# A fused attention, expert and scan layer on Trainium2: the scan norm adds its two halves on GpSimd, and every order list is replaced

## The reference

```
x = x + attention(LN(x))      # 16 heads of 8; elu(q)+1, elu(k)+1; weights = (rope q . rope k) / (q . k); no softmax
x = x + experts(LN(x))        # router, 2 of 8 experts, 512 hidden, exact gelu, plus a shared expert
x = x + scan(LN(x))           # 256 inner channels, 16 states
x = x + experts(LN(x))        # the same experts again
```

```
xc = silu(conv(W_in x));  dt = softplus(W_dt xc + b)
h  = exp(dt * A[s]) * h + dt * B[s] * xc       # for each of 16 states s, over time
y  = sum over s of C[s] * h
mu = mean(y);  var = mean((y - mu)**2)          # over the 256 channels
y  = (y - mu) * rsqrt(var + 1e-5) * ln_g + ln_b
out = W_out ((y + xc * D) * silu(z))
```

## Time and profile before

| | us |
|---|---|
| Median of 3 runs (lowest, highest) | 3752.46 (3748.87, 3768.64) |
| The profiled execution's own time | 3761.18 |
| Its span, first to last instruction | 3759.4 |
| PE busy | 3412.8 (91%) |
| ACT busy | 3189.4 (85%) |
| DVE busy | 2658.9 (71%) |
| POOL busy | 1330.1 (35%) |
| Granted TensorE clock, mean | 0.949 of full speed |

### The profile page before, as it was taken

The page is one execution under the profiler, slowest core; times in us unless marked ns, Lnnn a source line. Parts: engine busy times, 40 slices in busy tenths (PEclk is TensorE's granted clock), DMA queues, the critical chain, the costliest instruction groups (busy, mean ns, idle before and its releaser), DMA issues. The chain is left out here.

```text
span 3759.4 us, 38374 instructions
## 1 busy us (share of the span) xinstructions
PE 3412.8 (91%) x11446; PEld 1450.4 (39%) x11446; DVE 2658.9 (71%) x3527; ACT 3189.4 (85%) x4024; POOL 1330.1 (35%) x744
## 2 busy tenths in 40 slices
PE   5886999999999999999999999999999999998847
PEld 1231434444343444434343444434344343434424
DVE  4438768686776868687786868778686867768572
ACT  4776889999999999899999999899999989886643
POOL 0122434244343424334242434434243443315251
PEclk6796999999999999999999999999999999999968
DMA  5433445454545545464544545454454545434332
GB/s 161 122 84 110 138 152 157 140 179 134 178 136 163 163 132 182 128 196 138 159 151 147 174 134 178 143 159 151 140 174 138 182 146 163 149 108 165 117 128 76
DMA packets 214847, 552.01 MB, mean 147 GB/s; under 512 B 25105, under 2 KB 96626, under 8 KB 214642
## 3 DMA queue, kind: packets, MB, share of 16 engines
q1 hardware_dynamic: 212914, 547.99, 47.2%
q10 hardware_dynamic: 1728, 1.57, 0.1%
HBM read 488.65 MB, written 63.18 MB: 147 GB/s over the span
## 5 line engine op out<-in xcount | busy, mean ns | idle before, releaser
L938 PE MATMUL bank<-hF,wst 128*128 128x512 f32 x2304 | 1149.6, 620 | 30.4 <-ACT hF L1040 15.6
L1525 POOL TENSOR_TENSOR yM<-yM,ws 128x1024 f32<-128x1024 f32 x240 | 634.3, 2643 | 1410.4 <-DVE ws L1422 1407.2
L1303 DVE TENSOR_TENSOR rPool<-bank,rPool 128x512 f32<-128x512 f32 x1024 | 700.1, 686 | 550.4 <-PE bank L866 440.5
L1040 ACT ACTIVATE hF<-bank,cols 128x512 f32<-128x512 f32 x1152 | 772.3, 687 | 259.4 <-PE bank L927 245.3
L1194 ACT ACT_TABLE_LOAD x518 | 664.6, 1283 | 9.2
L1040 ACT ACTIVATE rPool<-bank 128x512 f32<-128x512 f32 x1024 | 571.9, 597 | 93.9 <-PE bank L861 87.5
L925 PE MATMUL bank<-xnH,wst 128*128 128x512 f32 x1152 | 605.4, 526 | 30.7 <-ACT hF L1040 20.2
L1415 DVE TENSOR_TENSOR_SCAN ws<-dAs,ws 128x1024 f32<-128x1024 f32 x256 | 600.9, 2353 | 7.4 <-ACT dAs L1040 0.8
L938 PEld LDWEIGHTS bank<-hF,wst 128*128 128x128 f32 x2304 | 419.9, 193 | 463.5 <-issue 364.2
L866 PE MATMUL bank<-qpk,kpk 48*128 48x512 bf16 x1024 | 412.2, 405 | 94.0 <-DVE rPool L1303 85.7
L1040 ACT ACTIVATE rPool<-rPool 128x2048 f32<-128x2048 f32 x256 | 490.4, 1916 | 2.3
(11 more groups left out here) (162 smaller groups left out, 2934.6 us busy)
## 6 DMA issues: line engine op xcount, KB each, us to landing
wst<-wscr SPq DMA_DIRECT2D x288, 768.0 KB, 5.8
bc<-bcscr SPq DMA_DIRECT2D x256, 512.0 KB, 4.4
cB<-gscr SPq DMA_DIRECT2D x256, 256.0 KB, 4.6
kpk<-kscr SPq DMA_DIRECT2D x128, 192.0 KB, 5.5
qpk<-qscr SPq DMA_DIRECT2D x128, 192.0 KB, 5.9
qscr<-parts SPq DMA_DIRECT2D x186, 128.0 KB, 2.2
kscr<-parts SPq DMA_DIRECT2D x186, 128.0 KB, 2.3
wscr<-wst SPq DMA_DIRECT2D x9, 512.0 KB, 6.2
```

What stands on the lines that cost most here:

```text
L938: pe.matmul(ps[FFN][:, :], w2, hF[:, (NCH * f + q) % HSLOTS, :], start=(c == 0), stop=(c == FC - 1)).then_inc(s_dn, 1)
L1040: return nc.scalar.activation(out_, in_, fn, **kw)
L1303: v.tensor_tensor(rP[:, slot, c, :], ps[num_bank(b, s)][:, :], rP[:, slot, c, :], ALU.mult).then_inc(s_mul, 1)
L1525: g.tensor_tensor(yM[:, :, :], yM[:, :, :], ws[:, s % 3, :, :], ALU.add).then_inc(s_ya, 1)
```

## The change

In the 15 norms of the passes 2 to 16, POOL adds the two halves first, and PE sends only the sum through `onesI`, for the mean and again for the variance. The sum goes to the first half of `sqE`. The last norm (pass 17) stays as it was. A new semaphore `s_E_half` counts the sums.

```
             def scan_norm(m, i, name):                       # PE
+                last = isinstance(i, int) and i == NB + 1
                 if name == "mean":
-                    pe.wait_ge(s_ya, floor((NS - 1) * (m + 1)))
+                    if last:
+                        pe.wait_ge(s_ya, (NS - 1) * NB)
+                    else:
+                        pe.wait_ge(s_E_half, floor(2 * m + 1))
...
-                    ones_mm(PRE, onesI, [yM[:, 0, :], yM[:, 1, :]], 2).then_inc(s_E_mean, 1)
+                    if last:
+                        ones_mm(PRE, onesI, [yM[:, 0, :], yM[:, 1, :]], 2).then_inc(s_E_mean, 1)
+                    else:
+                        ones_mm(PRE, onesI, [sqE[:, 0, :]]).then_inc(s_E_mean, 1)
                 elif name == "var":
-                    pe.wait_ge(s_E_sq, floor(m + 1))
-                    ones_mm(PRE, onesI, [sqE[:, 0, :], sqE[:, 1, :]], 2).then_inc(s_E_var, 1)
+                    if last:
+                        pe.wait_ge(s_E_sq, NB)
+                        ones_mm(PRE, onesI, [sqE[:, 0, :], sqE[:, 1, :]], 2).then_inc(s_E_var, 1)
+                    else:
+                        pe.wait_ge(s_E_half, floor(2 * m + 2))
+                        ones_mm(PRE, onesI, [sqE[:, 0, :]]).then_inc(s_E_var, 1)
...
+            def scan_norm(m, name):                          # POOL
+                if name == "mean":
+                    pool.wait_ge(s_ya, floor((NS - 1) * (m + 1)))
+                    pool.wait_ge(s_sc, floor(NS * (m + 1)))
+                    g.tensor_tensor(sqE[:, 0, :], yM[:, 0, :], yM[:, 1, :], ALU.add).then_inc(s_E_half, 1)
+                elif name == "var":
+                    pool.wait_ge(s_E_sq, floor(m + 1))
+                    g.tensor_tensor(sqE[:, 0, :], sqE[:, 0, :], sqE[:, 1, :], ALU.add).then_inc(s_E_half, 1)
```

All order lists are replaced. In `START` they differ widely: of PE's 691 items the two lists share about two thirds in order. In `MAIN` only some neighbours trade places. Two lines of it:

```
 MAIN POOL
-    H.add N.acc*2 H.add*3 N.acc*5 F.add P.rope F.add N.acc*2 P.rest F.add*2 P.rest*2 P.rope P.rest F.add*3 M.take
+    H.add N.acc*2 H.add*3 N.acc*5 F.add P.rope F.add N.acc*2 E.mean P.rest F.add E.var F.add P.rest*2 P.rope P.rest
```

More of the change, by code:

```diff
@@ L96 @@
+    2:G.up*2 2:A.den 2:A.num 2:G.down 2:A.den*2 2:A.num 2:A.den 2:G.down*2 2:A.den 2:A.num*2 2:A.av 2:A.num 2:G.up*4
+    2:G.down 2:A.den 2:G.down 2:A.num 2:A.den*2 2:A.num 2:G.up 2:A.den*2 2:A.num*2 2:G.up 2:A.av 2:G.down*3 2:G.up*2
+    2:A.num 2:G.down 2:A.num 2:G.up 2:A.den 2:A.num 2:A.den*2 2:A.num 2:G.up 2:G.down*2 2:A.den*2 2:A.num 2:A.den
+    2:A.num 2:G.down 2:A.num 2:A.av 2:G.down 2:A.num 2:G.up*2 2:A.num 2:G.up 2:A.num*2 2:A.av*2 2:G.up 2:A.close
 """,
     "ACT": """
-    -1:P.load -1:P.mean -1:P.var -1:S.acol -1:P.qk*4 -1:P.cast*2 -1:P.pk -1:P.cast*2 -1:P.pk -1:P.cast*3 -1:P.pk
@@ L123 @@
+    2:T.log 2:M.var 2:A.ex 2:M.xp 2:A.ln*2 2:M.xp 2:T.gelu 2:G.gelu*3 2:M.xp 2:G.gelu 2:T.silu 2:M.silu*2 2:M.xp
+    2:P.cast 2:M.silu*2 2:M.row 2:T.log 2:A.ln*2 2:M.dt 2:A.ex 2:A.ln 2:M.dt 2:A.ln 2:M.sp 2:T.gelu 2:G.gelu 2:T.log
+    2:A.ln*2 2:M.decay*2 2:A.ex 2:P.cast 2:A.ln*4 2:M.decay 2:A.ex 2:T.gelu 2:G.gelu*6 2:T.log 2:A.ln*4 2:A.ex
+    2:M.decay*2 2:T.gelu 2:G.gelu*2 2:P.cast 2:G.gelu*2 2:T.log 2:A.ln*4 2:A.ex 2:A.ln*4 2:A.ex 2:T.gelu 2:G.gelu*4
+    2:T.log 2:M.decay*2 2:A.oT
 """,
     "DVE": """
-    -1:S.early -1:P.mean -1:S.bias -1:P.var -1:P.til*2 -1:P.rope -1:P.til*2 -1:P.rest*2 -1:S.take -1:P.rest
@@ L141 @@
-    2:A.mul 2:G.part 2:A.mul 2:M.scan 2:A.mul*2 2:M.dbx 2:M.scan 2:M.hc*2 2:A.mul 2:G.part 2:A.mul*3 2:M.dbx*2
-    2:M.scan 2:M.hc 2:A.mul*3 2:G.part 2:A.mul 2:M.scan 2:A.mul*3 2:M.hc 2:A.mul*2 2:G.part 2:A.mul*3 2:M.dbx*2
+    -1:S.early -1:P.mean -1:S.bias -1:P.var -1:P.til*2 -1:P.rope -1:P.til*2 -1:P.rest*2 -1:S.take -1:P.rest*2
+    -1:P.rope 0:A.v -1:P.rest*3 0:W.split*3 -1:P.rest 0:A.mul*4 0:P.mean 0:A.mul*2 0:P.var 0:A.mul*6 0:W.split*2
+    0:P.til*2 0:A.mul*5 0:W.split 0:A.mul*3 0:W.split 0:A.mul*4 0:W.split 0:A.mul*4 0:P.til*2 0:A.mul*15 0:W.split
@@ L173 @@
+    A.den G.down A.num G.up A.den A.num A.den*2 A.num G.down*2 A.den*2 G.up A.num A.den*2 A.num A.av A.num G.down
+    A.num G.down A.num G.up*2 A.num G.up A.num A.av*2 G.up A.close
 """,
@@ L342 @@
+    16:M.scan 16:M.hc*2 16:G.part 16:M.dbx 16:M.scan 16:M.hc 16:G.part 16:M.dbx*2 16:M.scan*2 16:G.part 16:M.hc*2
+    16:M.dbx*2 16:M.scan*2 16:M.hc*2 16:G.part 16:M.dbx*2 16:M.scan 16:M.hc 16:M.scan 16:M.hc 17:E.mean 17:E.var
+    17:E.gate 17:G.mean 17:G.var 17:G.router 17:G.route 17:G.part 17:G.turn 17:G.part*8
 """,
     "POOL": """
-    14:H.add 14:N.acc*2 14:H.add*3 14:N.acc*5 14:F.add 14:P.rope 14:F.add 14:N.acc*2 14:P.rest 14:F.add*2
-    14:P.rest*2 14:P.rope 14:P.rest 14:F.add*3 14:M.take 14:P.rest*2 14:M.keep 14:M.acc 14:P.rest 14:G.add 14:P.rest
@@ L351 @@
+    16:G.add 16:M.acc*2 16:G.add 16:M.acc 16:G.add 16:M.acc*5 16:G.add 16:M.keep 16:G.add*3 16:M.acc*4 16:G.add
+    16:M.acc*2 17:G.add*8
 """,
```

403 lines of the change are left out of this document (198 added, 205 removed).

## The result

| | before | with the change |
|---|---|---|
| Median, us (lowest, highest, runs) | 3752.05 (3748.87, 3768.64, 4) | 3784.47 (3779.86, 3789.80, 4) |
| Profiled execution, us | 3761.18 | 3779.86 |
| Its span, us | 3759.4 | 3778.1 |

The ratio is 1.008, with a 95% interval of 1.0057 to 1.0104. The change makes the kernel 0.8% slower, some 30 us. The forecast was 3741 us with a range up to 3766, so the time went the other way and ended beyond the range.

A forecast was written before the change was run, and what follows sets the result against it. PE was taken to set the pace, busy 206.98 of 216.68 us per `MAIN` period. Gains of 5.2 (edit), 2 (`MAIN` lists) and 4 (`START`) made 11.2 us: 3752.5 to 3741 us, range 3718 to 3766.

The forecast's parts named there:

- the new lists: Changed instruction orders: trades in PE's `MAIN` gain 2 us in eleven passes, bounds 11 us both ways; `START` gains 4.
- START, 4 us of gain: The reordered part before the loop: a gain of 4 us, between a loss of 10 and a gain of 20.
- The one piece that was named: In `START`, a weight store issued ahead of the q and k loads now comes behind them: 1 us gained.
- The edit, 5.2 us of gain: Sums on POOL in 15 norms: 4.4 us in passes 3 to 15, 1.1 in pass 2, less 0.3 in pass 16.
- The ceiling of 25.5 us: All of PE's saved work, 30 x 0.85 us, kept without new waits; as a rival 3721 us with the lists, chance 0.12.
- The mean: Norm's first product: starts 1.41 us after the last `N.acc`; PE waits 0.76 us, saves 0.85, gains 0.09 a pass.
- The variance: Norm's second product: starts 1.41 us after ACT's square; waits 0.39 us, saves 0.85, and 0.25 a pass stays.
- The rival of slow sums: POOL's sums take 3.32 us each in place of 1.28, losing 53 us: 3806, or 3800 with the lists; chance 0.03.
- The rival in which `F.add` is first: Behind the variance's sum POOL's `F.add` precedes DVE's `P.til`, 0.94 us lost a pass: 3766, or 3760 with lists; chance 0.14.
- `P.rest` later by 1.3 us: POOL's delay falls into ACT's 0.94 us wait ahead of its third gelu, its cover: no cost, up to 0.3 a pass otherwise.
- Pass 2: PE comes 1.45 us after the last `N.acc`, so it doesn't wait at the mean: 1.1 us gained.
- pass 16: PE comes 0.05 us after the last `N.acc`, so the sum's 1.36 us count in full: 0.3 us lost.

The follow-up runs named there:

- pe_b: edit_only with, of PE's new `MAIN` list, only the stretch with `P.qk`, `num` and `down` reordered; 3782.28 us, ratio 1.0076 to before.
- pe_a: edit_only with, of PE's new `MAIN` list, only the first trade (a `den` after one `up` in place of two); 3752.96 us, ratio 1.0001 to before.
- pe_c: edit_only with, of PE's new `MAIN` list, only the three late trades of a `den` and a `num`; 3746.55 us, ratio 0.9983 to before.
- edit_only: The change's code with the order lists of before, POOL's two new items put in; 3740.66 us, ratio 0.998 to before.
- start_new: edit_only with the change's new `START` list alone; 3749.61 us, ratio 0.9992 to before.
- stretch_no_edit: The kernel before, in code and lists, with only the new `P.qk` stretch in PE's `MAIN`; 3784.52 us, ratio 1.008 to before.
- mean_later: edit_only with PE's mean product one `up` later in passes 2 to 15; 3761.94 us, ratio 1.0017 to before.
- finish_new: edit_only with the change's new `FINISH` list alone; 3747.72 us, ratio 0.9979 to before.
- main_back: The change with the lists of `MAIN` put back to those of before, POOL's new items kept; 3760.11 us, ratio 1.0022 to before.

## Why the prediction was wrong

**The failed step** is the one on the new lists: "In `MAIN` neighbours trade places at some fifteen spots of PE's list. Such a trade is worth at most the wait that it shortens", with "0.2 us per pass" of gain and "bounds of 1 us per pass on both sides". That bounds what a trade can win. It doesn't bound what it can lose, since a trade can make a wait where there was none. pe_b shows 25.1 us in ten periods, 2.5 per pass, from one stretch of four trades (there are eight in PE's `MAIN`, not fifteen: one in pe_a, four in pe_b, three in pe_c). By the runs the sum of the forecast reads: 7.5 us gained by the edit in place of 5.2, 22 us lost with `MAIN` in place of 2 gained, 16 us lost with `START` and `FINISH` in place of 4 gained, together 30 us lost. A price for the two waits could have been read from the trace of before, where two `num` follow each other further down in every pass:

```profile
952.17 0.39 PE L866 MATMUL bank<-qpk,kpk 48*128 48x512 bf16 x1
952.17 0.60 PE L861 MATMUL bank<-qpk,kpk 48*128 48x512 bf16 x2
953.34 0.39 PE L866 MATMUL bank<-qpk,kpk 48*128 48x512 bf16 x1 [0.57 <-DVE rPool L1303]
954.51 0.39 PE L866 MATMUL bank<-qpk,kpk 48*128 48x512 bf16 x1 [0.79 <-DVE rPool L1303]
```

With a plain `num` behind a `num` at 0.79 us and the order of the instructions after, the two new spots give 2 x 0.79 x 11 = 17 us by this estimate, and the forecast would have been near 3760. That has the sign right and is half of the 36 us between edit_only and pe_b.

**START, 4 us of gain: wrong, by sign.** The close of pass 2 ends what `START` orders. In the profiles with the edit and the old `START` (ten kernels) it starts at 557.3 to 566.0 us, mean 560.3; with the new one (five kernels, after among them) at 564.2 to 565.5, mean 564.9. Without the edit it is 569.1 and 560.4 old and 566.0 new. So by the profiles the new `START` costs about 4.6 us. PE isn't idle for longer there (115 to 116 us up to that close in both groups) but busy for 5 us longer, and the clock is at its lower level for 183 us against 178, so about half of it is the clock's. The medians of start_new and edit_only (0.12% apart) can't tell it from nothing. One execution would have told the opposite: after against before is 564.2 against 569.1. The two rows of one and the same `START`, code and lists alike up to there, in before and in stretch_no_edit:

```profile
0.00:569.12 569.12, 453.24 (x1469) 159.96 (x1469) 333.29 (x515) 420.63 (x543) 135.81 (x92) 0.83 0.43 129
```

```profile
0.00:560.41 560.41, 443.67 (x1469) 158.69 (x1469) 333.14 (x515) 420.48 (x543) 135.48 (x92) 0.85 0.44 131
```

PE is busy 9.6 us longer in the first at a granted clock of 0.83 against 0.85, with the same instructions. The one piece that was named went wrong as well. The loads of q and k don't wait for the weight store ahead of them:

```profile
42.53 2.06 SPq L716 DMA_DIRECT2D kscr<-parts  x3
46.66 0.33 SPq L729 DMA_DIRECT2D kpk<-kscr  x1
```

The first load goes out 2.07 us behind the end of the last write, against 45.73 - 43.63 = 2.10 before, with no store between. The first `den` is at 53.24 us, 0.88 later than in the earlier trace rows, since the writes themselves start 0.96 us later. `FINISH` was given nothing: from the close of pass 15 to the end it takes 361.9 us in the five profiles with the new one and the edit, 358.8 with the old (ten), 3 us lost, which the medians can't tell either.

**The edit, 5.2 us of gain: right in mechanism and within the error in size.** Measured are 7.5 us (1.5 to 13). The ceiling of 25.5 us wasn't reached: PE is busy 2077.86 - 2060.39 = 17.5 us less in ten periods of edit_only, as 20 x 0.85 says, and waits 9.9 us for POOL.

- The mean: start 1.40 us behind the data against 1.41 forecast, wait 0.68 against 0.76.
- The variance: 1.40 against 1.41. The next `num` starts 1990.84 - 1988.25 = 2.59 us behind the square against 2.69 forecast and 2.94 before.
- The sums: 1.27 us, not 3.3. The rival of slow sums is out.
- `P.til` and the second `F.add`: DVE starts at 1989.50, POOL at 1989.55, 0.05 us later. DVE takes its plain 0.68 us and POOL's sum 1.76 in place of 1.28. The rival in which `F.add` is first didn't come about in the change; in mean_later it did. By the Trainium skill, "SBUF — State Buffer", section "Who interferes with whom", who is first holds the ports and the other waits. The 1.76 us on POOL agree within 0.15 us: `P.til` ran for 0.63 us more when the sum started, and the sum took 0.48 us more.
- `P.rest` later by 1.3 us: ACT's cast waits 0.64 us for it at 1983.99, and the gelu behind it at 1984.70 doesn't wait at all, where it had waited 0.94. The cover held.
- Pass 2 has a wait of the mean now (0.64 us at 443.01), pass 16 has one of 0.10 us (3500.05): both the other way round than forecast. The lists did it: with the old ones (edit_only) it is none in pass 2 and 1.22 us in pass 16, as forecast; start_new has 0.65 in pass 2, finish_new 0.11 in pass 16. It is below what the medians can tell.

**What stays open.** start_new and finish_new lose 0.12% and nothing against edit_only, but both together (main_back) 0.42%, 16 us, of which the two ends explain 7.6. Its ten periods are:

```profile
783.48:2959.20 2175.72, 2071.16 (x7102) 883.96 (x7101) 1630.68 (x2151) 1993.51 (x2521) 868.97 (x490) 0.99 0.50 155
```

PE is busy for 10.8 us more there than in edit_only with the same code and the same `MAIN`, and idle for 1.7 more. In these ten periods the clock is granted at its lower level for 64.9 us, against 44.4 in edit_only; half of the difference is 10.2 us. (It is 47.8 in before and 61.4 in after.) The twelve executions of each say the same: their mean granted clock is 0.9502 in main_back and 0.9507 in start_new, 0.9525 in edit_only and 0.9524 in finish_new. 0.0023 of a span of 3757 us is 8.6 us, an estimate, and 8.4 were missing, itself no more than the medians can tell. So the rest fits the clock, which is lower in the two kernels with the new `START`. Why the clock is lower behind another `START` wasn't found. Nor is it settled where the part of the 18 us comes from that the waits for `A.mul` don't give when both trades are there.

## What to carry to other kernels

When a change comes with a new instruction order, price the order like an edit: go through the trades on the engine that sets the pace, look for two neighbours of which the second needs what another engine makes of the first, and take the wait for it from a place where the same pair already stands. A trade wins at most the wait that it shortens, but it can cost a whole wait, in every pass. Look at trades in pairs too: two `num` became neighbours only by two of them. Where a move shifts one engine by a tenth of a microsecond, look which two others meet there. And compare the parts of a program over several profiles before a difference of 5 us at its start is put down to anything.

## What the runs showed of the hardware

**The clock falls at the same two places.** In the ten periods of after it is granted at half (1.2 GHz) in 14 stretches, each some 3.4 or 6.8 us long; 8 begin about 41 us behind a close and 6 about 169 us behind, both right after PE has waited or between two waits (for ACT ahead of the norm of P, for `A.mul`). One of them as a window, and PE just ahead of it:

```profile
1045.50:1048.90 3.40, 3.40 (x7) 0.96 (x6) 2.40 (x4) 3.40 (x6) 2.14 (x1) 0.54 0.66 215
```

```profile
1043.29 0.87 PE L865 MATMUL bank<-qpk,kpk 48*128 48x512 bf16 x2 [0.76 <-ACT rPool L1055]
1044.75 1.63 PE L821 MATMUL bank<-xP,onesD 128*128 128x512 f32 x2 [0.59 <-ACT xP L1055]
```

The clock column is the last but two. Two waits of 0.76 and 0.59 us end at 1044.75, and the same kind of product as in the earlier trace rows takes 1.63 us in place of 1.13. At half the clock a stretch of 3.4 us costs some 1.7 us, an estimate, more than the 1.35 us of the two waits ahead of it. In before too ten of eleven falls are there, but not in each pass, so the same code differs from pass to pass.

**Who gets the ports turns on nanoseconds.** DVE's product of the gate (L1454, 128x1024 from two SBUF tiles) and POOL's `P.rest` start at the same recorded time in pass 9 of after:

```profile
1996.80 2.24 DVE L1454 TENSOR_TENSOR yM<-yM,zs 128x1024 f32<-128x1024 f32 x1
```

```profile
1996.80 1.17 POOL L1515 TENSOR_TENSOR til<-til,parts 128x512 f32<-128x512 f32 x1 [4.37 <-ACT parts L1055]
```

and in edit_only:

```profile
1970.24 1.22 DVE L1449 TENSOR_TENSOR yM<-yM,zs 128x1024 f32<-128x1024 f32 x1
```

```profile
1970.24 2.25 POOL L1510 TENSOR_TENSOR til<-til,parts 128x512 f32<-128x512 f32 x1 [4.36 <-ACT parts L1050]
```

In the one DVE takes 2.24 us in place of 1.22, in the other POOL 2.25 in place of 1.17. The loser stands for about the winner's whole time, and the starts in hundredths of a microsecond don't say who it will be. The trace has them in nanoseconds. Of the 212 such meetings within 20 ns in the eighteen profiles POOL loses all 108 in which its record starts behind DVE's or at most 4 ns ahead, DVE loses all 58 in which POOL's is 7 ns or more ahead, and at 5 and 6 ns it is 23 to 23.
